# The end of an attention stage, written out as one sequence per engine, in a one-core Trainium2 kernel

## The chip, the cores and the metric

The kernel runs on one core of one Trainium2 chip. The metric is the device time of one execution in microseconds; the median of 3 runs of the kernel before is 155.03 us (154.98 to 155.16). The profiled execution is a fourth one, with its own time.

## The reference

A transformer block over 8 batches of 128 tokens of 256 floats: normalise, attend (8 heads), add, normalise again, route each token to one of 8 experts, and add the routed and a shared feed-forward layer.

```
x = x + attention(layernorm(x), ctx, ctx, lengths)
    # x is (8, 128, 256): the 128 rows are 8 heads of 16, the 256 columns are queries and keys
    # per batch and head: softmax(scale * log(length) * q^T k) applied to v
x = x + shared(layernorm(x)) + gate * expert(layernorm(x))
```

There are 64 heads in all (8 batches of 8), and each head's scores are a 256 by 256 matrix with an inner size of 16.

## The kernel before

Every engine has its own instruction list; semaphores order them. The attention is a software pipeline over steps `t`. In step t, up to 31, TensorE (PE) makes the raw scores of heads 2t and 2t+1 (`scores`, line 1021); VectorE (DVE) takes the maximum of each row of them (`maximum`, line 558). Seven steps later (`LAG`) PE makes the scores of the same two heads again, transposed and with the maximum subtracted (`shifted_scores`, line 1042), and ScalarE (ACT) takes the exponential out of PSUM (`exponentials`, line 813). PE then weighs the values of four heads, one half of the keys at a time (`weigh_values(m, c)`, line 1058). Every float32 matrix product is two matmul instructions, so that one call of `shifted_scores` (a head, one half of the keys) is two of them and one call of `weigh_values` is eight. A head's scores use 32 of the 128 rows of the PE array, and consecutive heads use different row groups; a head of the values uses 32 columns.

After the two halves of a batch's heads are weighed comes a chain that hands the batch from engine to engine: `copy_output` (ACT, 819), `turn_output` (PE, 1072), `scale_output` (DVE, 566 and 571), `turn_back` (PE, 1084), `add_attention` (DVE, 580), `token_stats` (DVE, 585 and 587), `token_rstd` (ACT, 823 and 825), `token_norm` (GpSimd, POOL, 428 and 431, for the batches up to 5; DVE, 591, for the last two), `turn_tokens` (PE, 1095), `high_tokens` (ACT, 829) and `low_tokens` (DVE, 596). `turn_output`, `turn_back` and `turn_tokens` of all batches but the last write one PSUM bank, X, so each waits until what the one before it left there has been read (`x_free`, which sorts them by the steps in OUT_TURN, OUT_BACK and TTURN). POOL also splits expert weights into high and low parts (`split_expert(n)`, lines 451 and 453), one of eight per step from t = 32 on.

Raw scores go through banks 0 to 2, shifted scores through banks 3 to 5 in turn. The raw scores end with t = 31, so that the steps from 32 to 39 hold the shifted scores of two heads each and no raw ones. One loop, `for t in range(TAIL)`, issues all steps on each engine; each looks up in lists by t which calls a step has. On PE the last steps are these: step 33 has `weigh_values(11, 1)`, shifted 52 and 53, `turn_tokens(3)`; 34 `weigh_values(12, 0)`, shifted 54 and 55, `turn_output(5)`; 35 `weigh_values(12, 1)`, 56 and 57, `turn_back(5)`; 36 `weigh_values(13, 0)`, 58 and 59, `turn_tokens(4)`; 37 `weigh_values(13, 1)`, 60 and 61, `turn_tokens(5)`; 38 `weigh_values(14, 0)`, 62 and 63, `turn_output(6)`; 39 `weigh_values(14, 1)`, (15, 0), (15, 1), `turn_back(6)`, `shared_up(0, 0)`; 40 `turn_output(7)`, `shared_up(0, 1)`; 41 `turn_tokens(6)`. The shared layer (`shared_up`, lines 1122 and 1123) and the experts follow.

Of the kernel before, what the change touches and what calls it, by code (L numbers as in the profile page):

```python
# [39 lines left out]
ACT = mybir.ActivationFunctionType  # L40
AX_X = mybir.AxisListType.X

P = 128
# [13 lines left out]
NS = 3  # L57
# [46 lines left out]
def tokens_at(shifted, offset, last):  # L104

    return shifted + [4 * b + offset for b in range(SHIFTED, B - 1)] + [END + last]
# [2 lines left out]
STATS = tokens_at([4 * b + LAG + 9 for b in range(SHIFTED)], LAG + 8, 7)  # L109
TRSTD = tokens_at([4 * b + LAG + 10 for b in range(SHIFTED)], LAG + 9, 8)  # L110
TNORM = tokens_at([4 * b + LAG + 11 for b in range(SHIFTED)], LAG + 9, 9)
TTURN = tokens_at([4 * b + LAG + 14 for b in range(SHIFTED - 1)] + [TURNS + 4], LAG + 10, 10)
THI, TLOW = TTURN, TTURN
TAIL = END + 3


SHARED_SPLIT = 14
# [37 lines left out]
def block_kernel(nc, x, ctx_in, lens, wg, w1, w3, w2, sw1, sw3, sw2, consts, out):  # L155
    with ExitStack() as es:
# [95 lines left out]


        bank = [es.enter_context(nc.psum_tensor(f"bank{i}", [P, 512], F32)) for i in range(8)]
        mx_bank, sc_bank, O, X = bank[0:NS], bank[NS:2 * NS], bank[6], bank[7]
        turned_out, back = X[:].rearrange("p (u h e) -> p u h e", u=2, h=H), X[:, 0:D]
        u1_bank, u3_bank = (bank[0], bank[3], bank[2]), (bank[1], bank[4], bank[5])
        eu1_bank, eu3_bank = (bank[3], bank[0]), (bank[4], bank[1])
# [134 lines left out]
        def _(pool):  # L393
# [49 lines left out]
            def split_expert(n):  # L443

                e, i = divmod(n, len(UP_PIECES))
                a, z = UP_PIECES[i]
                if i == 0:
                    pool.wait_ge(ld_w[e], 32)
                if n == 0:
                    pool.wait_ge(shifted, (B - 2) * H)  # L450
                nc.gpsimd.tensor_copy(ehi[e][:, a:z], whole[e][:, a:z]).then_inc(ew_hi_pool, 1)
                pool.wait_ge(ew_hi_pool, n + 1)
                nc.gpsimd.tensor_tensor(elo[e][:, a:z], whole[e][:, a:z], ehi[e][:, a:z].bitcast(F32),  # L453
                                        ALU.subtract).then_inc(ew_lo_pool, 1)

            for t in range(TAIL):
                for i, begin in LATE.items():
                    if t == begin:
                        for b in range(*CHUNKS[i]):
                            keys(b)  # L460
                    if t == begin + 1:
                        for b in range(*CHUNKS[i]):
                            queries(b, 0)
                            queries(b, 1)
                if t in TNORM[:B - 2]:
                    token_norm(TNORM.index(t))
                i, rest = divmod(t - SHARED_SPLIT, 3)
                if rest == 0 and 0 <= i < len(SHARED_PIECES):
                    split_shared(i)
                if 0 <= t - EXPERT_SPLIT < 2 * len(UP_PIECES):  # L470
                    split_expert(t - EXPERT_SPLIT)


            def send_rows(part):
# [35 lines left out]
        def _(dve):  # L510
# [143 lines left out]
                nc.vector.tensor_tensor(sig[k % 3][0:rows], u3_bank[UP_BANK[k]][0:rows, :], sig[k % 3][0:rows],  # L654
                                        ALU.mult).then_inc(h_made, 1)

            for t in range(TAIL):
                if t < TURNS:
                    maximum(2 * t)
                    maximum(2 * t + 1)  # L660
                if t == 1:
                    query_scales(1)
                    eager_queries(1)
                if t == LAG + 2:
                    nc.vector.tensor_copy(trib[:], cst[:, TRI:TRI + P]).then_inc(cst_copied, 1)
                    nc.vector.tensor_copy(x2[:, :, D:D + 1].bitcast(U32),
                                          cst[:, NUMBER:OWN].unsqueeze(2)).then_inc(numbered, 1)
                for i, begin in LATE.items():
                    if t == begin:
                        query_stats(i)  # L670
                    if t == begin + 1:
                        query_scales(i)
                for when, work in ((OUT_SCALE, scale_output), (OUT_ADD, add_attention), (STATS, token_stats),
                                     (TNORM[B - 2:], token_norm), (TLOW[:B - 2], low_tokens)):
                    if t in when:
                        work(when.index(t) + (B - 2 if work is token_norm else 0))
                if t == TURNS:
                    dve.wait_ge(v_turned, B // 2)
                    dve.wait_ge(k_eager, 2 * EAGER)
                    dve.wait_ge(k_made, 2 * (B - EAGER))  # L680
                    nc.vector.memset(lgt[3 * ROWS:P], 0.0).then_inc(lgt_set, 1)
# [36 lines left out]
            def expert_out(e):  # L718
# [2 lines left out]
                nc.vector.scalar_tensor_tensor(res[:, e, :], y_bank[(e + 1) % 2][:, 0:D], xe[:, e, D + 1:DW],  # L721
                                               res[:, e, :], ALU.mult, ALU.add).then_inc(e_out, 1)

            scale_output(B - 1)
            low_tokens(B - 2)
            add_attention(B - 1)
# [44 lines left out]
        def _(act):  # L771
# [36 lines left out]
            def exponentials(n):  # L808
                g = n // 4
                act.wait_ge(shifted, n + 1)  # L810
                if g >= NPT:
                    act.wait_ge(valued, g - NPT + 1)
                nc.scalar.activation(pt[:, g % NPT, n % 4, :], sc_bank[n % NS][:], ACT.Exp).then_inc(exped, 1)  # L813

            def copy_output(b):
                act.wait_ge(valued, 2 * b + 2)
# [49 lines left out]
            eager_keys(0)  # L866
            query_rstd(1)
            eager_keys(1)
            for t in range(TAIL):
                if t == MROW[0]:  # L870
                    maxima_rows(0)
                for i, begin in LATE.items():
                    if t == begin + 1:
                        query_rstd(i)
                if t in VALUES:
                    values(VALUES.index(t))
                if t in OUT_COPY:
                    copy_output(OUT_COPY.index(t))
                if 0 <= t - LAG < TURNS:
                    exponentials(2 * (t - LAG))  # L880
                if t in MROW[1:]:
                    maxima_rows(MROW.index(t))
                if t in THI[:B - 2]:
                    high_tokens(THI.index(t))
                if 0 <= t - LAG < TURNS:
                    exponentials(2 * (t - LAG) + 1)
                if t in TRSTD:
                    token_rstd(TRSTD.index(t))

            def expert_high(e, k):  # L890

# [66 lines left out]
        def _(pe):  # L958
# [74 lines left out]
            def shifted_scores(n, c):  # L1033

                b, half, rows = place(n)
                if n < NS and c == 0:
                    pe.wait_ge(maxed, FIRST - NS + n + 1)
                if n % H == 0 and c == 0:
                    pe.wait_ge(ld_m[b % 2], 32 * ring_pass(b, 2))
                if n >= NS and c == 0:  # L1040
                    pe.wait_ge(exped, n - NS + 1)
                mm = nc.tensor.matmul(sc_bank[n % NS][:, c * D:(c + 1) * D], kz[rows, b, half, c * P:(c + 1) * P],  # L1042
                                      qz[rows, b, half, :], start=True, stop=True)
                if c == 1:
                    mm.then_inc(shifted, 1)
# [108 lines left out]
                                          start=False, stop=(b == z - 2), skip_group_check=True)  # L1154
                mm.then_inc(pos_done, 1)

            for t in range(TAIL):
                if t == END + 1:
                    turn_output(B - 1)
                    shared_up(0, 1)  # L1160
                for m in range(NG):
                    for c in range(2):
                        if t == WEIGH[m][c]:
                            weigh_values(m, c)
                if t < LAG and t % 2 == 0:
                    first_half, heads = range(2), range(2 * t, min(2 * t + 4, 2 * LAG))
                    if t == 0:
                        for u in range(2):
                            for n in first_half:
                                scores(n, u)  # L1170
                        heads = range(2, 4)
                    for u in range(2):
                        for n in heads:
                            scores(n, u)
                for part in range(2):
                    for k in range(2):
                        if LAG <= t < TURNS:
                            scores(2 * t + k, part)
                        if 0 <= t - LAG < TURNS:
                            shifted_scores(2 * (t - LAG) + k, part)  # L1180
                if t == MROW[0]:
                    turn_maxima(0)
                if t in VALUES:
                    turn_values(VALUES.index(t))
                if t in UNREAD:
                    unread(t)
                for when, work in ((MROW[1:], turn_maxima), (OUT_TURN, turn_output), (OUT_BACK, turn_back),
                                     (TTURN, turn_tokens)):
                    if t in when:
                        work(when.index(t) + (1 if work is turn_maxima else 0))  # L1190

                if t == END:
                    shared_up(0, 0)

            def shared_down(b):

# [63 lines left out]
            def expert_down(e):  # L1260
# [10 lines left out]
                                          start=(c == 0), stop=(c == FC - 1))  # L1271
                mm.then_inc(e_down, 1)

            turn_back(B - 1)
            shared_up(1, 0)
            shared_up(1, 1)
# [50 lines left out]
```

## Time and profile before

| | |
|---|---|
| median of 3 runs | 155.03 us (154.98 to 155.16) |
| profiled execution, own time | 156.0 us |
| span of the profile | 154.1 us |
| busy: PE, DVE, ACT, POOL | 143.4, 99.3, 82.7, 67.2 us |
| the last shifted scores and values | about 71 to 86 us of the span |

The span runs from the first to the last instruction; the execution's own time is 1.9 us more. Busy time of PE is modelled by the ends of pipelined matmuls, so a full PE row says that it always had work begun, not that it worked at its peak. The kernel's pace is read from the starts of consecutive instructions.

### The profile page before, as it was taken

Reading aid. Unit: us, or ns where it says so; the run is one execution under the profiler, and the core shown is the slowest. Engines: PE = TensorE matmul, PEld = TensorE weight load, DVE = VectorE, ACT = ScalarE, POOL = GpSimd, SP = SyncE. Lnnn points to the kernel's source line nnn. Section 1 sums busy time; section 2 is a strip of 40 time slices with the busy share of each in tenths; the row PEclk is TensorE's granted clock in tenths of the full one; section 3 lists DMA queues with packets and bytes.
Section 4 is the critical chain, followed back from the end, with each engine's and each line's share of the span. In section 5 each row is a group of like instructions: output and inputs, shape, how many; then the busy total and the mean of one; then the engine's idle time right before and its main releaser. Section 6 shows DMA issues by size and latency. Waiting matters only on the chain.

```text
span 154.1 us, 3410 instructions
## 1 busy us (share of the span) xinstructions
PE 143.4 (93%) x1254; PEld 97.1 (63%) x1254; DVE 99.3 (64%) x232; ACT 82.7 (54%) x179; POOL 67.2 (44%) x100
## 2 busy tenths in 40 slices
PE   7799999998999999999998999999999999899930
PEld 2364565553655555555544677688999998899720
DVE  0589886688878888884232456887674484875220
ACT  3444265765848595767676248554503665762300
POOL 7115849303830508071639600276600777272350
PEclk9999999999999999999999999999999999999996
DMA  2992635362353500000800089722467532121010
GB/s 71 354 359 89 169 118 185 104 194 93 85 200 110 170 6 0 2 6 2 277 3 4 2 271 338 239 102 70 154 194 182 172 92 67 34 94 37 33 62 34
DMA packets 15824, 18.42 MB, mean 120 GB/s; under 512 B 1980, under 2 KB 15077, under 8 KB 15808
## 3 DMA queue, kind: packets, MB, share of 16 engines
q1 hardware_dynamic: 14368, 14.98, 30.6%
q0 software_dynamic: 1152, 2.97, 5.9%
q10 hardware_dynamic: 288, 0.26, 0.6%
q8 instruction: 10, 0.16, 0.4%
q14 instruction: 6, 0.05, 0.1%
HBM read 14.12 MB, written 4.21 MB: 119 GB/s over the span
## 4 chain that ended last, share of the span: by engine, by line
PE 84%; DVE 4%; issue 3%; DMA 2%; ACT 2%; POOL 2%; SPq 0%; DVEq 0%; POOLq 0%
PE bank L1021 19%; PE bank L1058 11%; PE bank L1210 6%; PE bank L1122 6%; PE bank L1042 6%; PE bank L1269 6%; PE bank L1123 5%; PE bank L1245 5%; PE bank L1244 4%; PE bank L973 3%; PE bank L1072 3%; DMA xs<-in_x 2%; PE bank L1084 2%; PE bank L1095 2%; PE bank L1030 2%
## 5 line engine op out<-in xcount | busy, mean ns | idle before, releaser
L558 DVE TENSOR_REDUCE nm<-bank 128x2 f32<-128x512 f32 x64 | 40.9, 686 | 10.0 <-PE bank L1021 9.5
L813 ACT ACTIVATE pt<-bank 128x512 f32<-128x512 f32 x64 | 36.2, 596 | 19.4 <-PE bank L1042 19.1
L1042 PE MATMUL bank<-qz,kz 32*128 32x256 f32 x256 | 37.9, 400 | 0.0
L1021 PE MATMUL bank<-kz,qz 32*128 32x256 f32 x256 | 34.6, 400 | 1.1 <-DVE qz L535 1.1
L1021 PEld LDWEIGHTS bank<-kz,qz 32*128 32x128 f32 x256 | 21.9, 184 | 13.5 <-DVE nm L558 5.8
L1042 PEld LDWEIGHTS bank<-qz,kz 32*128 32x128 f32 x256 | 23.5, 184 | 3.4 <-ACT pt L813 2.2
L1058 PE MATMUL bank<-pt,vext 128*32 128x256 f32 x256 | 20.2, 390 | 0.1
L403 POOL TENSOR_SCALAR qz<-xs,rs,mrs 128x256 f32<-128x256 f32 x14 | 7.7, 560 | 20.1 <-DVE mrs L529 20.1
L482 POOL DMA_INDIRECT expert_rows<-rk,idx_s x8 | 8.7, 1090 | 14.7 <-DVE idx_s L635 12.9
L497 POOL DMA_INDIRECT xs<-out,rk x8 | 8.8, 1099 | 11.1 <-DMA out<-xs 9.0
L504 POOL DMA_INDIRECT out<-xs,rk x8 | 8.4, 1048 | 11.3 <-DVE xs L721 6.9
L428 POOL TENSOR_SCALAR mrs<-mv,rstd 128x1 f32<-128x1 f32 x6 | 1.6, 260 | 23.4 <-ACT rstd L825 23.4
L973 PE MATMUL bank<-onesb 128*128 128x512 bf16 x34 | 10.7, 450 | 1.0 <-POOL onesb L397 1.0
L1058 PEld LDWEIGHTS bank<-pt,vext 128*32 128x32 f32 x256 | 5.2, 108 | 7.1 <-issue 5.7
L596 DVE TENSOR_TENSOR xlo<-bank,xhi 128x256 fp32r<-128x256 f32 x8 | 3.4, 422 | 8.1 <-ACT xhi L829 8.1
L715 DVE TENSOR_TENSOR qz_rest<-bank,late 128x352 f32<-128x352 f32 x8 | 4.2, 522 | 6.0 <-ACT late L919 4.7
L1269 PE MATMUL bank<-wraw,kz_rest 128*128 128x256 f32 (+1 forms) x30 | 7.4, 384 | 0.5 <-DVE rlo L708 0.5
L919 ACT ACTIVATE late<-bank 128x352 f32<-128x352 f32 x8 | 3.7, 466 | 7.6 <-PE bank L1245 6.9
L453 POOL TENSOR_TENSOR ew<-wraw,ew 128x352 fp32r<-128x352 f32 x8 | 7.5, 934 | 0.7
L973 PEld LDWEIGHTS bank<-onesb 128*128 128x128 bf16 x34 | 3.4, 112 | 5.9 <-issue 3.6
L1210 PE MATMUL bank<-shi,hThi 128*128 128x256 f32 (+1 forms) x24 | 7.0, 293 | 0.1
L1210 PE MATMUL bank<-shi,hTlo 128*128 128x256 f32 (+1 forms) x24 | 6.8, 282 | 0.0
(153 smaller groups left out, 301.3 us busy)
## 6 DMA issues: line engine op xcount, KB each, us to landing
wraw<-in_w SPq DMA_DIRECT2D x10, 352.0 KB, 3.4
wlate<-in_w SPq DMA_DIRECT2D x6, 352.0 KB, 4.2
wraw<-in_w SPq DMA_DIRECT2D x10, 128.0 KB, 3.4
expert_rows<-zero SPq DMA_DIRECT2D x1, 1032.0 KB, 6.7
out<-xs SPq DMA_DIRECT2D x8, 128.0 KB
xs<-in_x SPq DMA_DIRECT2D x3, 256.0 KB, 4.9
cs<-in_ctx SPq DMA_DIRECT2D x3, 256.0 KB, 5.1
wlate<-in_w SPq DMA_DIRECT2D x6, 128.0 KB, 3.9
```

The costliest lines, as they stand in the source:

```text
L482: nc.gpsimd.indirect_dma_start(xd_dram, bass.IndirectOffsetOnAxis(ap=idx_s[:, b:b + 1], axis=0), x2[:, b, :], None, bounds_check=E * C - 1 ...
L497: nc.gpsimd.indirect_dma_start(res[:, e, :], None, out_rows, number(e), bounds_check=B * P - 1, oob_is_err=False).then_inc(gathered[e], 16)
L504: nc.gpsimd.indirect_dma_start(out_rows, number(e), res[:, e, :], None, bounds_check=B * P - 1, oob_is_err=False).then_inc(out_sent, 16)
L558: nc.vector.tensor_reduce(nm[:, b % 2, :, place], scores_bank[:].rearrange("p (u c) -> p u c", u=2), AX_X, ALU.max, negate=True).then_inc( ...
L813: nc.scalar.activation(pt[:, g % NPT, n % 4, :], sc_bank[n % NS][:], ACT.Exp).then_inc(exped, 1)
L973: nc.tensor.matmul(X[:].rearrange("p (n c) -> p n c", c=P), onesb[:], onesb[:].unsqueeze(1).broadcast_to([P, 4, P]), start=True, stop=True)
L1021: mm = nc.tensor.matmul(scores_bank[:, u * D:(u + 1) * D], qz[rows, b, half, u * P:(u + 1) * P], kz[rows, b, half, :], start=True, stop=True)
L1042: mm = nc.tensor.matmul(sc_bank[n % NS][:, c * D:(c + 1) * D], kz[rows, b, half, c * P:(c + 1) * P], qz[rows, b, half, :], start=True, sto ...
L1058: mm = nc.tensor.matmul(O[32 * j:32 * j + 32, g * D:(g + 1) * D], vext[:, b, c, h, :], pt[:, m % NPT, i, c * D:(c + 1) * D], start=(c == 0 ...
L1122: nc.tensor.matmul(u1, weights(part, S1 + f * P, F + WG, c, n1), tokens, start=a, stop=z)
L1210: mm = nc.tensor.matmul(base_bank[b % 2][:, 0:D], hpart[0:rows, half, f, j * P:(j + 1) * P], part[0:rows, S2 + f * D:S2 + (f + 1) * D], st ...
L1269: mm = nc.tensor.matmul(y_bank[(e + 1) % 2][:, 0:D], hTe[0:rows, e % 2, c * P:(c + 1) * P], down_at[e][c][0:rows], start=(c == 0), stop=(c ...
```

## The change

The step loops of all engines now end after step 32 (`STEADY`). What came after is written out call by call for PE, ACT, DVE and POOL. On PE the last twelve heads' shifted scores (52 to 63) are issued in three groups of four heads, first half of the keys of all four, then the second half; they use the banks 4, 1, 2, 0, 5, 3 in turn, so banks of the raw scores too. The key halves of the values of groups 13, 14 and 15 of four heads stand together. On POOL `split_expert(1)` to `(6)` come ahead of `token_norm(4)`. `turn_tokens(5)` comes after `turn_back(6)`.

```diff
-TTURN = tokens_at([4 * b + LAG + 14 for b in range(SHIFTED - 1)] + [TURNS + 4], LAG + 10, 10)
+TTURN = [4 * b + LAG + 14 for b in range(SHIFTED - 1)] + [TURNS + 4, END + 1, END + 2]
-TAIL = END + 3
+STEADY = TURNS + 1
+FOURS = 2 * (STEADY - LAG)
+FOURS_BANKS = (4, 1, 2, 0, 5, 3)
+def shifted_bank(n):
+    return NS + n % NS if n < FOURS else FOURS_BANKS[(n - FOURS) % len(FOURS_BANKS)]
+def banks_last_head(n):
+    return next((k for k in range(n - 1, -1, -1) if shifted_bank(k) == shifted_bank(n)), None)
...
 # POOL, after the loop
+            for n in range(1, 7):
+                split_expert(n)
+            token_norm(B - 4)
+            split_expert(7)
+            token_norm(B - 3)
...
 # DVE, after the loop
+            low_tokens(3)
+            scale_output(5)
+            add_attention(5)
+            token_stats(5)
+            low_tokens(4)
+            scale_output(6)
+            add_attention(6)
+            token_stats(6)
+            low_tokens(5)
+            token_norm(6)
             scale_output(B - 1)
             low_tokens(B - 2)
...
 # ACT, after the loop
+            copy_output(5)
+            exponentials(52)
+            high_tokens(3)
+            exponentials(53)
+            exponentials(54)
+            exponentials(55)
+            token_rstd(4)
+            exponentials(56)
+            exponentials(57)
+            copy_output(6)
+            token_rstd(5)
+            exponentials(58)
+            high_tokens(4)
+            for n in range(59, NH):
+                exponentials(n)
+            token_rstd(6)
+            high_tokens(5)
+            copy_output(B - 1)
...
 # PE, in shifted_scores
-                if n >= NS and c == 0:
-                    pe.wait_ge(exped, n - NS + 1)
+                last = banks_last_head(n)
+                if last is not None and c == 0:
+                    pe.wait_ge(exped, last + 1)
+                if n >= FOURS and shifted_bank(n) < NS and c == 0:
+                    pe.wait_ge(maxed, NH)
...
+            def four_shifted(n):
+                for part in range(2):
+                    for k in range(4):
+                        shifted_scores(n + k, part)
...
 # PE, after the loop
+            weigh_values(11, 1)
+            four_shifted(52)
+            turn_tokens(3)
+            weigh_values(12, 0)
+            turn_output(5)
+            weigh_values(12, 1)
+            four_shifted(56)
+            turn_back(5)
+            weigh_values(13, 0)
+            weigh_values(13, 1)
+            turn_tokens(4)
+            four_shifted(60)
+            turn_output(6)
+            weigh_values(14, 0)
+            weigh_values(14, 1)
+            turn_back(6)
+            turn_tokens(5)
+            weigh_values(15, 0)
+            weigh_values(15, 1)
+            shared_up(0, 0)
+            turn_output(B - 1)
+            shared_up(0, 1)
+            turn_tokens(6)
             turn_back(B - 1)
```

## Rows read from the trace of the kernel before

**Rows 1.** The page: the chain that ended last, by engine.
```profile
PE 84%; DVE 4%; issue 3%; DMA 2%; ACT 2%; POOL 2%; SPq 0%; DVEq 0%; POOLq 0%
```

**Rows 2.** PE in order of time, the tail: start, duration, what, idle before it.
```profile
71.30 1.13 PE L1042 MATMUL bank<-qz,kz 32*128 32x256 f32 x8
72.36 0.44 PE L1095 MATMUL bank<-cst,rk 128*128 128x128 f32 x2
72.74 0.64 PE L1058 MATMUL bank<-pt,vext 128*32 128x256 f32 x8
73.31 1.13 PE L1042 MATMUL bank<-qz,kz 32*128 32x256 f32 x8
74.37 0.66 PE L1072 MATMUL bank<-cst,osum 128*128 128x128 f32 x4
74.96 0.64 PE L1058 MATMUL bank<-pt,vext 128*32 128x256 f32 x8
...
81.54 0.44 PE L1095 MATMUL bank<-cst,rk 128*128 128x128 f32 x2 [0.88 <-POOL rk L431]
...
85.78 0.44 PE L1084 MATMUL bank<-cst,att 128*128 128x128 f32 x2
85.97 0.48 PE L1122 MATMUL bank<-xhi,shi 128*104 128x512 f32 x1
...
87.47 0.60 PE L1072 MATMUL bank<-cst,osum 128*128 128x128 f32 x4
```

**Rows 3.** The same list in a steady step: first score matmul, and what follows all 16.
```profile
65.11 0.48 PE L1021 MATMUL bank<-kz,qz 32*128 32x256 f32 x1
...
66.19 0.55 PE L1072 MATMUL bank<-cst,osum 128*128 128x128 f32 x3
```

**Rows 4.** The chain that ended last: start, duration, what; the last two value halves.
```profile
84.78 1.07 PE bank L1058 x16
```

**Rows 5.** ACT in order of time in the tail.
```profile
72.96 0.37 ACT L829 CAST xhi<-bank 128x256 fp32r<-128x256 f32 x1
73.21 0.62 ACT L813 ACTIVATE pt<-bank 128x512 f32<-128x512 f32 x1
...
74.47 1.09 ACT L813 ACTIVATE pt<-bank 128x512 f32<-128x512 f32 x2 [0.22 <-PE bank L1042]
...
79.92 0.31 ACT L823 ACTIVATE lnv<-mv,epst 128x1 f32<-128x1 f32 x1
...
80.37 0.57 ACT L819 COPY osum<-bank 128x512 f32<-128x512 f32 x1
80.84 0.60 ACT L813 ACTIVATE pt<-bank 128x512 f32<-128x512 f32 x1
...
85.92 0.59 ACT L819 COPY osum<-bank 128x512 f32<-128x512 f32 x1 [1.19 <-PE bank L1058]
```

**Rows 6.** DVE in order of time in the tail.
```profile
73.36 0.42 DVE L596 TENSOR_TENSOR xlo<-bank,xhi 128x256 fp32r<-128x256 f32 x1 [1.91 <-ACT xhi L829]
...
75.36 0.42 DVE L571 TENSOR_TENSOR att<-bank,rinv 128x256 f32<-128x256 f32 x1
...
86.26 0.42 DVE L580 TENSOR_TENSOR xs<-bank,xs 128x256 f32<-128x256 f32 x1 [1.30 <-PE bank L1084]
```

**Rows 7.** POOL in order of time: two weight splits, and one norm of tokens.
```profile
67.04 0.48 POOL L451 CAST ew<-wraw 128x352 fp32r<-128x352 f32 x1
...
68.48 0.47 POOL L451 CAST ew<-wraw 128x352 fp32r<-128x352 f32 x1
...
80.57 0.26 POOL L428 TENSOR_SCALAR mrs<-mv,rstd 128x1 f32<-128x1 f32 x1 [2.44 <-ACT rstd L825]
80.93 0.56 POOL L431 TENSOR_SCALAR rk<-xs,rstd,mrs 128x256 f32<-128x256 f32 x1
```

**Rows 8.** Busy time by stretch: length, each engine's busy us, PE clock, DMA.
```profile
80.00:82.00 2.00, 1.12 (x14) 0.53 (x14) 0.01 (x1) 1.41 (x5) 1.25 (x4) 1.00 0.00 0
...
140.00:154.00 14.00, 7.62 (x42) 6.40 (x40) 2.84 (x6) 1.81 (x4) 3.89 (x4) 0.92 0.11 37
```

More of the change, by code:

```diff
@@ L254, in block_kernel @@
         bank = [es.enter_context(nc.psum_tensor(f"bank{i}", [P, 512], F32)) for i in range(8)]
-        mx_bank, sc_bank, O, X = bank[0:NS], bank[NS:2 * NS], bank[6], bank[7]
+        O, X = bank[6], bank[7]
         turned_out, back = X[:].rearrange("p (u h e) -> p u h e", u=2, h=H), X[:, 0:D]
@@ L454, in split_expert @@
                                         ALU.subtract).then_inc(ew_lo_pool, 1)
-            for t in range(TAIL):
+            for t in range(STEADY):
                 for i, begin in LATE.items():
@@ L471, in _ @@
                     split_expert(t - EXPERT_SPLIT)
+            for n in range(1, 7):
[3 more added lines that the diff above has]
+            token_norm(B - 3)
+            for n in range(8, 2 * len(UP_PIECES)):
+                split_expert(n)
             def send_rows(part):
@@ L655, in shared_hidden @@
                                         ALU.mult).then_inc(h_made, 1)
-            for t in range(TAIL):
+            for t in range(STEADY):
                 if t < TURNS:
@@ L812, in exponentials @@
                     act.wait_ge(valued, g - NPT + 1)
-                nc.scalar.activation(pt[:, g % NPT, n % 4, :], sc_bank[n % NS][:], ACT.Exp).then_inc(exped, 1)
+                nc.scalar.activation(pt[:, g % NPT, n % 4, :], bank[shifted_bank(n)][:], ACT.Exp).then_inc(exped, 1)
             def copy_output(b):
@@ L868, in _ @@
             eager_keys(1)
-            for t in range(TAIL):
+            for t in range(STEADY):
                 if t == MROW[0]:
@@ L1039, in shifted_scores @@
                     pe.wait_ge(ld_m[b % 2], 32 * ring_pass(b, 2))
-                if n >= NS and c == 0:
-                    pe.wait_ge(exped, n - NS + 1)
-                mm = nc.tensor.matmul(sc_bank[n % NS][:, c * D:(c + 1) * D], kz[rows, b, half, c * P:(c + 1) * P],
+                last = banks_last_head(n)
[3 more added lines that the diff above has]
+                    pe.wait_ge(maxed, NH)
+                mm = nc.tensor.matmul(bank[shifted_bank(n)][:, c * D:(c + 1) * D], kz[rows, b, half, c * P:(c + 1) * P],
                                       qz[rows, b, half, :], start=True, stop=True)
@@ L1155, in count_tokens @@
                 mm.then_inc(pos_done, 1)
[L1157 to L1160, printed above, removed]
+            for t in range(STEADY):
                 for m in range(NG):
@@ L1190, in _ @@
                         work(when.index(t) + (1 if work is turn_maxima else 0))
-                if t == END:
-                    shared_up(0, 0)
+            def four_shifted(n):
+                for part in range(2):
+                    for k in range(4):
+                        shifted_scores(n + k, part)
             def shared_down(b):
```

## The prediction

> **What bounds the kernel now.** I read the page first, for the engine that carries the chain of waits. The reader is to see that PE holds 84% of it and the DMA 2% [rows 1]: what shortens PE's list, or its idle time, shortens the kernel, as long as nothing else becomes late. Then I read the instructions in order of time, engine by engine, from 70 to 88 us, since averages over the kernel say nothing about this stretch. In it PE is never without work but once: it stands 0.88 us before `turn_tokens(5)` for POOL's normed tokens [rows 2]. The other engines wait for it: the exponentials of two heads take ACT 1.09 us [rows 5], while the two heads' scores and what stands between them and the next pair take PE about 2 us (71.30 to 73.31, 73.31 to 75.53) [rows 2].
>
> The step of most weight is a ratio of two rows. In the tail one pair of heads is 8 matmul instructions and takes 72.36 - 71.30 = 1.06 us [rows 2]. In a steady step 16 instructions (two raw, two shifted heads, in four row groups) take 66.19 - 65.11 = 1.08 us [rows 3]. PE runs as many row groups at once as it is given, and the tail gives it two of four.
>
> **The change part by part.** All times are on the span's own scale; differences of starts are used, not durations, because matmuls overlap.
>
> *Shifted scores.* Six pairs at 1.06 = 6.36 us go, three groups of four come. The trace has no group of four shifted heads. From below a group costs no less than the pair's 1.06, from above two pairs, 2.12. I take 1.08, the steady step, which has the same shapes, the same four row groups and four banks [rows 3]. Gain 3.12 us of PE work.
>
> *Key halves together.* One half with its neighbours is 75.53 - 74.96 = 0.57 us [rows 2]; the last two, which stand together already, take 85.78 - 84.78 = 1.00 [rows 2, 4]. Groups 13 and 14 come together: 2 x (1.14 - 1.00) = 0.28 us less. Their bounds are 0 and 0.28; I take 1.00 for each.
>
> *The turns.* As many as before: `turn_output` 74.96 - 74.37 = 0.59, `turn_tokens` and `turn_back` 0.38 (72.74 - 72.36) [rows 2]. They are what is late next, since the chain that hands a batch from engine to engine has not become shorter and PE now comes to its links earlier. So the gain isn't the sum of the two terms above, and I lay the new order out from 71.30, where both kernels start their first tail scores.
>
> First group 71.30 to 72.38; `turn_tokens(3)` to 72.75; values (12, 0) to 73.32. `turn_output(5)` waits for `low_tokens(3)`. That chain begins with the first exponential, 1.18 us after the group's start (a pair's is 74.47 - 73.31 = 1.16 [rows 2, 5], four heads end some hundredths later), so at 72.48; `high_tokens(3)` 0.49 later (an exponential's share of the 1.09 [rows 5]) at 72.97; `low_tokens(3)` 0.40 after that (73.36 - 72.96) and 0.42 long [rows 5, 6]: 73.79. With 0.05 for the hand-over to PE (as 81.54 after 80.93 + 0.56 [rows 2, 7]) PE goes on at 73.84: **first gap 0.52**.
>
> `turn_output(5)` to 74.43, values (12, 1) to 75.00, second group to 76.08 (heads 56 to 59 wait for exponentials up to 53, over by 74.2, and for the maxima of batch 7, sent in the last loop step), `turn_back(5)` to 76.46, values 13 to 77.46. `turn_tokens(4)` waits for POOL. POOL's second split starts at 68.48; a split takes 68.48 - 67.04 = 1.44; six of them now stand ahead of `token_norm(4)`, which takes 0.92 (80.57 to 81.49) [rows 7]. So 68.48 + 6 x 1.44 + 0.92 + 0.05 = 78.09: **second gap 0.63**. `token_rstd(4)` is over by 75.3 (exponentials 52 to 55 and one copy from 72.48), so the splits, and not ACT, are the price here. Behind the waiting `turn_tokens(4)` stand the last group and all values; ACT waits for neither then, as it still has exponentials 58 and 59.
>
> `turn_tokens(4)` to 78.47, last group to 79.55. On ACT: exponential 56 at 76.18, 57 at 76.67, `copy_output(6)` 1.14 after values 13 began (85.92 - 84.78 [rows 4, 5]), at 77.60, 0.47 long to its follower, `token_rstd(5)` 0.45 (80.37 - 79.92 [rows 5]), exponential 58 at 78.52, `high_tokens(4)` at 79.01, `low_tokens(4)` done at 79.83. `turn_output(6)` at 79.88: **third gap 0.33**. It ends at 80.47, values 14 at 81.47; the scaled output is ready 1.41 after the turn's start (75.36 + 0.42 - 74.37 [rows 2, 6]), at 81.29, in time. `turn_back(6)` 81.47. `turn_tokens(5)` now stands right behind it in the same bank and must wait for `add_attention(6)`, 0.48 later (86.26 - 85.78) and 0.42 long [rows 2, 6], with the hand-over 82.42: **fourth gap 0.57**. To 82.80; values 15 to 83.80 (exponential 63 is over at 81.8: five at 0.49 from 79.26, and 0.60).
>
> `shared_up(0, 0)` then takes 87.47 - 85.97 = 1.50 [rows 2], so `turn_output(7)` starts at 85.30 (`copy_output(7)`, 1.14 after 82.80, is over at 84.5) against 87.47: **2.2 us earlier**. The same sum as a balance: PE work falls by 3.12 + 0.28, less 0.06 for rounding and a `turn_back` that no longer overlaps its follower; the one gap of 0.88 goes and four of 2.05 together come: about 2.2.
>
> *Waits added.* A group in a bank of the raw scores waits for the last maximum; the DVE's maxima end with step 31 and the first group is in step 33. Priced at nothing; had it to wait, everything on PE would. *POOL* ends its splits before 81, where it ended them at 87.2; the experts need them 30 us later. *After the tail* the order is the same on each engine, and expert loads, sends, stores and gathers all hang on instructions of the PE list (the load of expert 5 on `turn_output(7)`), so they move with it. I carry the whole 2.2 to the end.
>
> *A rule of the skill.* The exponentials, copies and norms of the tail are, from 72.48, 12 x 0.49 + 2 x 0.25 + 2 x 0.45 + 0.47 = 7.75 us of ACT (the `high_tokens` step is 73.21 - 72.96 [rows 5]), so ACT alone would be through at 80.3 and PE, waiting only for it, at 81.3. The Trainium skill (TensorEngine Tiling, "PSUM Bottleneck") says that after a fourfold tiling speed-up the copies out of PSUM may become the bound. By that rule ACT sets the tail and the kernel would gain about 4 us; by the rows ACT idles and the batch's chain sets it. No sum above uses the rule.
>
> **Time.** The profiled execution took 156.0 us with a span of 154.1; its outside part, 1.9, doesn't change, so it would be 153.8. The median shown is 155.03, 1.0 below that execution, and on this scale the forecast is 155.03 - 2.2 = 152.8 us.
>
> **The rivals.**
>
> *The gaps are hidden.* If the four links come in time, PE's own work sets the tail: 2.05 less idle, up to 150.8; with half of them 151.8. For it: each gap is 0.3 to 0.6 us, made of hand-overs that I added one by one. Against: they are rows, not guesses, and POOL's has one fixed start.
>
> *Given back later.* A transfer that doesn't move with PE (gathers, stores, weights of experts 5 to 7) takes half: 153.9. For it: the last 14 us have PE busy for only 7.62 [rows 8]. Against: DMA is 2% of the chain [rows 1].
>
> *The change doesn't do what it says.* Shifted heads don't run four wide, and a group costs 2.12. Laid out the same way the gap before `turn_output(5)` stays 0.5, POOL's is covered, the one before `turn_tokens(5)` stays, and values 15 end at about 85.9: 155.0, no change. Against: the steady step [rows 3].
>
> *Slower.* Four gaps in 9 us make PE's clock fall from 2.4 to 1.2 GHz (granted clock 1.00 to 0.5). From the second gap on, 78 to 84 us, 4.8 us of work would cost 4.8 more: 157.6. It decides once more than 2.2 us of work run at half rate. For it: where PE is busy for about half of 14 us the granted clock's mean is 0.92 [rows 8]. The Trainium skill (TensorE: Matmul & The Clock Gate, "What's actually happening") says that throttled is the default state and activity releases it. Against: a stretch with 0.88 of 2.00 us idle kept 1.00 [rows 8], and no new gap is as long.
>
> **How the numbers follow.** Forecast 0.70 (own range 152.3 to 153.3), gaps hidden 0.11, given back 0.09, not four wide 0.04, slower by the clock 0.05, other 0.01. The range, 151.8 to 154.1, takes in the forecast, half of the gaps hidden and half of the gain given back. A measurement of this kernel tells 0.2% (0.3 us) from no change. Faster 0.90, same 0.05, slower 0.05.
>
> **What would show it.** Right: three lots of 16 shifted matmul instructions, each about 1.08 us to PE's next start; PE idle before four turns, released by DVE, POOL, DVE, DVE, by 0.5, 0.6, 0.3 and 0.6; `token_norm(4)` at about 77.1; `turn_output(7)` at 85.3. Wrong: a group near 2 us, a granted clock under 1.00 between 76 and 90, or a chain of waits that leaves PE for DMA after 110 us.

## The result, and the profile after

The changed kernel takes 153.03 us (median of 4, 152.96 to 153.07) against 155.01 us for the kernel before (154.98 to 155.16): 1.98 us less, ratio 0.986 with a 95% interval of 0.9826 to 0.9893. Forecast were 152.8 us and a gain of 2.2. Times scattered on the occasion of the first four experiments below (the kernel before took 155.19 to 161.04 us there), so those four are judged by the length of the tail in their profile and not by their median. The profiled execution took 153.0 us, its span is 151.1.

PE in order of time, the changed kernel's tail (start, duration, what, idle before it). The same list of the kernel before is in [rows 2].

```profile
70.59 0.64 PE L1110 MATMUL bank<-pt,vext 128*32 128x256 f32 x8
71.16 1.15 PE L1094 MATMUL bank<-qz,kz 32*128 32x256 f32 x16
72.24 0.44 PE L1147 MATMUL bank<-cst,rk 128*128 128x128 f32 x2
72.61 0.64 PE L1110 MATMUL bank<-pt,vext 128*32 128x256 f32 x8
73.79 0.63 PE L1124 MATMUL bank<-cst,osum 128*128 128x128 f32 x4 [0.54 <-DVE xlo L616]
...
77.95 0.44 PE L1147 MATMUL bank<-cst,rk 128*128 128x128 f32 x2 [0.51 <-POOL rk L443]
78.31 1.15 PE L1094 MATMUL bank<-qz,kz 32*128 32x256 f32 x16
79.86 0.63 PE L1124 MATMUL bank<-cst,osum 128*128 128x128 f32 x4 [0.41 <-DVE xlo L616]
80.42 1.07 PE L1110 MATMUL bank<-pt,vext 128*32 128x256 f32 x16
81.42 0.44 PE L1136 MATMUL bank<-cst,att 128*128 128x128 f32 x2
82.47 0.41 PE L1147 MATMUL bank<-cst,rk 128*128 128x128 f32 x2 [0.61 <-DVE xs L600]
82.81 1.07 PE L1110 MATMUL bank<-pt,vext 128*32 128x256 f32 x16
...
85.29 0.60 PE L1124 MATMUL bank<-cst,osum 128*128 128x128 f32 x4
```

The reader is to see three things. A group of four heads is 16 matmul instructions in 72.24 - 71.16 = 1.08 us, where two heads took 1.06 [rows 2]. PE stands before four turns, released by DVE, POOL, DVE, DVE. And `turn_output(7)` starts at 85.29, 14.13 us after the first tail group, against 87.47 - 71.30 = 16.17 [rows 2]: 2.04 us less, which is the whole measured gain.

The rows that set these four releases, DVE and POOL in order of time:

```profile
73.22 0.42 DVE L616 TENSOR_TENSOR xlo<-bank,xhi 128x256 fp32r<-128x256 f32 x1 [1.91 <-ACT xhi L859]
...
79.29 0.42 DVE L616 TENSOR_TENSOR xlo<-bank,xhi 128x256 fp32r<-128x256 f32 x1 [1.72 <-ACT xhi L859]
...
81.90 0.42 DVE L600 TENSOR_TENSOR xs<-bank,xs 128x256 f32<-128x256 f32 x1 [0.65 <-PE bank L1136]
```

```profile
76.98 0.26 POOL L440 TENSOR_SCALAR mrs<-mv,rstd 128x1 f32<-128x1 f32 x1
77.33 0.56 POOL L443 TENSOR_SCALAR rk<-xs,rstd,mrs 128x256 f32<-128x256 f32 x1
```

The stretch that holds the first gap and the one that holds the other three (length, PE, PE load, DVE, ACT, POOL busy, granted clock, DMA share, GB/s) both keep a granted clock of 1.00, the 2.4 GHz level, as the stretch with the old gap did [rows 8]:

```profile
70.00:75.00 5.00, 4.46 (x56) 2.00 (x52) 2.03 (x6) 4.43 (x11) 4.68 (x8) 1.00 0.27 75
76.00:90.00 14.00, 12.47 (x111) 8.06 (x108) 6.06 (x19) 8.10 (x21) 3.89 (x7) 1.00 0.29 91
```

After the tail, the chain that ended last (start, duration, what; first the kernel before, then the changed one). The prediction named a chain that leaves PE for DMA after 110 us as a sign of being wrong, and the chain does that here: DMA has 4% of it now, against 2% before. The first expert rows land just as PE gets to them. But PE's own wait for them is short (the last row below: 0.15 us), and the stretch from the first `shared_down` to `turn_rows(0)` is not longer: 115.03 - 107.05 = 7.98 us before, 112.71 - 104.87 = 7.84 after.

```profile
107.05 4.47 PE bank L1210 x36
111.58 3.45 PE bank L1210 x27
115.03 0.37 PE bank L1225 x2
...
129.23 0.48 DVE xs L721
129.71 1.19 issue
130.90 0.44 DVE rlo L708
```

```profile
104.87 4.49 PE bank L1262 x36
...
110.60 2.06 DMA rk<-expert_rows
112.71 0.44 PE bank L1277 x2
```

```profile
112.71 0.44 PE L1277 MATMUL bank<-cst,rk 128*128 128x128 f32 x2 [0.15 <-DMA rk<-expert_rows]
```

The spans differ by 3.0 us and not by 2.0. Of the other 1.0 us, 0.14 lies ahead of the tail (`weigh_values(11, 1)` starts at 70.73 before and 70.59 after) and 0.8 behind it, in the experts: the profiled execution of before has 1.19 us in its chain in which DVE waited for nothing that the profile shows, and was itself 1.0 us over the median. From `turn_output(7)` to the end of the span it took 66.6 us, the changed kernel 65.8. Profiles of other kernels below show either length (65.8 to 66.3, or 66.8), whatever was edited, so this isn't the change's.

### The profile page after: what moved, and what is told of

It reads as the page before. It is cut to its first block, busy times and chain, and to the rows that moved or that the text cites. A ratio compares the mean times of both kernels' runs of the same rounds, so it can differ in the third digit from the quotient of the medians.

```text
span 151.1 us, 3413 instructions
## 1 busy us (share of the span) xinstructions
PE 139.9 (93%) x1254; PEld 95.4 (63%) x1254; DVE 99.3 (66%) x232; ACT 82.1 (54%) x179; POOL 67.9 (45%) x100
## 4 chain that ended last, share of the span: by engine, by line
PE 83%; DVE 4%; DMA 4%; issue 3%; ACT 2%; POOL 1%; SPq 0%; ACTq 0%; POOLq 0%; DVEq 0%
PE bank L1070 20%; PE bank L1110 11%; PE bank L1321 6%; PE bank L1174 6%; PE bank L1175 6%; PE bank L1297 5%; PE bank L1296 5%; PE bank L1262 4%; PE bank L1094 4%; PE bank L1022 3%; PE bank L1124 3%; DMA xs<-in_x 2%; PE bank L1136 2%; PE bank L1079 2%; PE bank L1308 2%
## 5 line engine op out<-in xcount | busy, mean ns | idle before, releaser
L843 ACT ACTIVATE pt<-bank 128x512 f32<-128x512 f32 x64 | 35.6, 597 | 17.4 <-PE bank L1094 17.3
L1094 PE MATMUL bank<-qz,kz 32*128 32x256 f32 x256 | 34.6, 400 | 0.0
L1094 PEld LDWEIGHTS bank<-qz,kz 32*128 32x128 f32 x256 | 21.6, 184 | 1.7 <-ACT pt L843 1.0
L517 POOL DMA_INDIRECT xs<-out,rk x8 | 9.9, 1235 | 12.0 <-DMA out<-xs 9.8
```

The lines of the kernel that those rows point to most:

```text
L517: nc.gpsimd.indirect_dma_start(res[:, e, :], None, out_rows, number(e), bounds_check=B * P - 1, oob_is_err=False).then_inc(gathered[e], 16)
L843: nc.scalar.activation(pt[:, g % NPT, n % 4, :], bank[shifted_bank(n)][:], ACT.Exp).then_inc(exped, 1)
L1094: mm = nc.tensor.matmul(bank[shifted_bank(n)][:, c * D:(c + 1) * D], kz[rows, b, half, c * P:(c + 1) * P], qz[rows, b, half, :], start=Tru ...
```

## The experiments

Each row of this table is one profile and one series of times. "Tail" runs from the start of `weigh_values(11, 1)` to the start of `turn_output(7)` on PE, "rest" from there to the end of the span. The first four experiments (two_wide to gaps_closed) are judged by the tail, the others by both. The last column compares with the kernel before as it ran on the same occasion, and not with the 155.01 us of the first row.

| kernel | tail, us | rest, us | median, us | against before (95%) |
|---|---|---|---|---|
| before | 87.47 - 70.73 = 16.74 | 66.6 | 155.01 | |
| changed | 85.29 - 70.59 = 14.70 | 65.8 | 153.03 | 0.986 (0.9826 to 0.9893) |
| two_wide | 85.48 - 70.78 = 14.70 | 66.8 | 153.46 | 0.975 (0.970 to 0.980) |
| fours_alone | 85.21 - 70.77 = 14.44 | 66.0 | 153.08 | 0.974 (0.969 to 0.980) |
| norm_early | 85.42 - 70.72 = 14.70 | 66.8 | 153.73 | 0.977 (0.971 to 0.983) |
| gaps_closed | 83.65 - 70.60 = 13.05 | 66.3 | 152.02 | 0.966 (0.961 to 0.971) |
| changed_again | 85.35 - 70.64 = 14.71 | 66.0 | 153.08 | 0.985 (0.982 to 0.989) |
| pairs_apart | 86.98 - 70.73 = 16.25 | 65.9 | 154.69 | 0.996 (0.994 to 0.998) |
| waits_swapped | 85.09 - 70.58 = 14.51 | 66.1 | 152.98 | 0.985 (0.981 to 0.988) |
| tokens5_late | 84.50 - 70.61 = 13.89 | 66.0 | 152.24 | 0.980 (0.976 to 0.983) |
| gaps_closed_again | 83.55 - 70.49 = 13.06 | 65.9 | 151.44 | 0.974 (0.969 to 0.978) |
| chain_first | 83.24 - 70.60 = 12.64 | 65.9 | 151.06 | 0.974 (0.968 to 0.980) |

**changed_again** is the changed kernel itself on another occasion.

> The changed kernel, unedited, as the common base of these runs. Both theories: from the start of weigh_values(11, 1) to turn_output(7) 14.70 us, as in its first profile; 153.0 us if nothing after the tail is late.

It repeated its tail within 0.01 us and its time within 0.05.

### Does the width carry the gain?

**two_wide**, each group as two pairs directly behind each other:

```diff
             def four_shifted(n):
-                for part in range(2):
-                    for k in range(4):
-                        shifted_scores(n + k, part)
+                for first in (n, n + 2):
+                    for part in range(2):
+                        for k in range(2):
+                            shifted_scores(first + k, part)
```

> Theory (the width of the shifted scores carries the gain): with two heads at a time in the same places a group costs 2 x 1.06 = 2.12 us instead of 1.08, three groups 3.1 us more PE work, of which POOL's gap before turn_tokens(4) and part of the one before turn_output(6) are covered: 2.1 us slower than the changed kernel, about 155.0 us. Rival (the order and the value halves carry it): within 0.5 us of 153.0.

The expectation failed, and by its number the rival was right: the tail is that of the changed kernel. PE in order of time shows why:

```profile
71.35 1.16 PE L1094 MATMUL bank<-qz,kz 32*128 32x256 f32 x16
72.44 0.44 PE L1147 MATMUL bank<-cst,rk 128*128 128x128 f32 x2
```

The 16 instructions took 1.09 us, not 2.12. The edit had not made them two wide: the second pair uses the other two row groups and ran beside the first without being interleaved with it. A stretch of 0.15 us at the start of the group (71.25 to 71.40) has four of them under way, all begun in it:

```profile
71.35 0.51 PE L1094 MATMUL bank<-qz,kz 32*128 32x256 f32 x4
```

So the run left the question open.

**pairs_apart**, the same pairs with a turn or a half of values between them:

```diff
-            four_shifted(52)
+            two_shifted(52)
             turn_tokens(3)
+            two_shifted(54)
...
+            two_shifted(56)
             weigh_values(12, 1)
-            four_shifted(56)
+            two_shifted(58)
...
+            two_shifted(60)
             turn_tokens(4)
-            four_shifted(60)
+            two_shifted(62)
```

> The changed kernel with each group of four taken apart into two pairs with a turn or a half of values between them (52, 53 / turn_tokens(3) / 54, 55; 56, 57 / weigh_values(12, 1) / 58, 59; 60, 61 / turn_tokens(4) / 62, 63). Theory (what saves the time is that 16 matmul instructions over four row groups follow each other, in whatever order): a pair alone costs 1.06 again, turn_output(7) starts 1.9 us later than in the changed kernel (16.6 after weigh_values(11, 1)), about 154.9 us. Rival (a group's saving comes from elsewhere, such as fewer exchanges with ACT): within 0.5 us of the changed kernel, as two adjacent pairs were.

PE in order of time:

```profile
71.30 1.13 PE L1094 MATMUL bank<-qz,kz 32*128 32x256 f32 x8
72.36 0.44 PE L1147 MATMUL bank<-cst,rk 128*128 128x128 f32 x2
72.73 1.13 PE L1094 MATMUL bank<-qz,kz 32*128 32x256 f32 x8
73.80 0.64 PE L1110 MATMUL bank<-pt,vext 128*32 128x256 f32 x8
74.37 0.66 PE L1124 MATMUL bank<-cst,osum 128*128 128x128 f32 x4
```

A pair takes 72.36 - 71.30 = 1.06 again, and the kernel 154.69 us, 1.61 more than the changed one beside it (tail 1.54 more; 1.9 was expected). The 3.1 us of additional PE work fill the gaps that the changed kernel has, all but the one before `turn_tokens(5)`: there is none before `turn_output(5)` here. In the same 0.15 us at its start a pair has two instructions under way, where two_wide has four:

```profile
71.30 0.48 PE L1094 MATMUL bank<-qz,kz 32*128 32x256 f32 x2
```

That four heads next to each other make the groups cheap is shown, and the order within the group doesn't matter. The banks that the pairs use are those of the change, so that the new banks alone don't give the gain. But each head has both a row group and a bank of its own, and no run parts the two: that it is the row groups and not the four banks written side by side is my reading. Two adjacent pairs in the same row groups, which would tell, were not tried. Against the kernel before, the new order with pairs is still 0.49 us shorter in the tail (16.25 against 16.74).

**fours_alone** takes the groups of four and leaves all other calls, on all engines, in the order of the kernel before:

```diff
 # POOL
-            for n in range(1, 7):
-                split_expert(n)
-            token_norm(B - 4)
-            split_expert(7)
-            token_norm(B - 3)
-            for n in range(8, 2 * len(UP_PIECES)):
+            split_expert(1)
+            token_norm(4)
+            split_expert(2)
+            split_expert(3)
+            token_norm(5)
+            for n in range(4, 8):
                 split_expert(n)
...
 # PE
             weigh_values(13, 0)
+            turn_tokens(4)
             weigh_values(13, 1)
-            turn_tokens(4)
             four_shifted(60)
+            turn_tokens(5)
+            weigh_values(14, 0)
             turn_output(6)
-            weigh_values(14, 0)
             weigh_values(14, 1)
-            turn_back(6)
-            turn_tokens(5)
             weigh_values(15, 0)
             weigh_values(15, 1)
+            turn_back(6)
             shared_up(0, 0)
...
 # and ACT's and DVE's calls in the order of the kernel before
```

> Groups of four and their banks, with all other calls of ACT, DVE and POOL in the order of the kernel before, and PE's turns and values as there too. Theory (the width alone carries the gain, the rest of the new order is worth nothing): laid out from the rows, PE stands before turn_output(5) by 0.6, before turn_tokens(5) and turn_output(6) by 0.6 and 0.5, turn_output(7) starts within 0.3 of the changed kernel's 85.3: 152.9 us (152.6 to 153.3). Rival (the new order is needed to make use of the groups): 154 us or more.

PE in order of time, from the third group on:

```profile
78.12 1.15 PE L1093 MATMUL bank<-qz,kz 32*128 32x256 f32 x16
80.07 0.44 PE L1146 MATMUL bank<-cst,rk 128*128 128x128 f32 x2 [0.81 <-POOL rk L443]
80.44 0.64 PE L1109 MATMUL bank<-pt,vext 128*32 128x256 f32 x8
81.52 0.63 PE L1123 MATMUL bank<-cst,osum 128*128 128x128 f32 x4 [0.44 <-DVE xlo L616]
82.08 1.50 PE L1109 MATMUL bank<-pt,vext 128*32 128x256 f32 x24
83.51 0.44 PE L1135 MATMUL bank<-cst,att 128*128 128x128 f32 x2
```

The theory holds, and more than that: the tail is 0.26 us shorter than with the whole change. It has three gaps (0.54, 0.81, 0.44) where the whole change has four. The four-head groups carry all of the gain, and by the tails the new order of the rest costs a little beside them. The medians (153.08 us here, 153.03 and 153.08 for the changed kernel on other occasions) don't tell the two apart.

### What are the gaps worth?

**norm_early**, POOL's `token_norm(4)` after split 4:

```diff
-            for n in range(1, 7):
+            for n in range(1, 5):
                 split_expert(n)
             token_norm(B - 4)
-            split_expert(7)
+            for n in range(5, 8):
+                split_expert(n)
...
```

> The changed kernel with POOL's token_norm(4) after split 4 and not after split 6. Theory: the gap before turn_tokens(4) goes (0.5 us), but turn_output(6) waits for low_tokens(4), which hangs on copy_output(6), token_rstd(5) and exponential 58 on ACT, not on POOL: its gap grows from 0.4 to 1.0 and the time stays at 153.0 (within 0.1). Rival (each gap of PE is worth its length): 152.5.

PE in order of time:

```profile
77.50 0.44 PE L1146 MATMUL bank<-cst,rk 128*128 128x128 f32 x2
77.86 1.15 PE L1093 MATMUL bank<-qz,kz 32*128 32x256 f32 x16
79.99 0.63 PE L1123 MATMUL bank<-cst,osum 128*128 128x128 f32 x4 [0.99 <-DVE xlo L615]
```

The turn starts without a gap, `turn_output(6)` waits 0.99 instead of 0.41, and the tail stays at 14.70. The median, 153.73, missed the expected 153.0: the tail bears the theory out, the time doesn't. The gap that was removed is worth nothing in the tail, since the next one hangs on another engine's list.

**tokens5_late**, `turn_tokens(5)` after `shared_up(0, 0)`:

```diff
             turn_back(6)
-            turn_tokens(5)
             weigh_values(15, 0)
             weigh_values(15, 1)
             shared_up(0, 0)
+            turn_tokens(5)
             turn_output(B - 1)
...
 # ACT
+            copy_output(B - 1)
             token_rstd(6)
             high_tokens(5)
-            copy_output(B - 1)
```

> The changed kernel with turn_tokens(5) after shared_up(0, 0) and copy_output(7) ahead of token_rstd(6) on ACT. Theory: only the gap before turn_tokens(5) goes (0.68 us), values 15 start right behind turn_back(6) as exponential 63 is just over; with a cheaper place for the turn turn_output(7) starts 0.8 us earlier: 152.2 us. Rival: the gap moves to values 15 or to turn_output(7) and the time stays at 153.0.

PE in order of time:

```profile
81.44 0.44 PE L1136 MATMUL bank<-cst,att 128*128 128x128 f32 x2
81.80 1.07 PE L1110 MATMUL bank<-pt,vext 128*32 128x256 f32 x16
```

Values 15 follow `turn_back(6)` at once. The tail is 0.82 us shorter, the time 0.84: as laid out. This gap came with the change's own order, two links of the chain directly behind each other.

**gaps_closed** moves all links ahead of what can wait:

```diff
 # ACT
             copy_output(5)
-            exponentials(52)
             high_tokens(3)
-            exponentials(53)
-            exponentials(54)
-            exponentials(55)
+            for n in range(52, 56):
+                exponentials(n)
...
             copy_output(6)
+            high_tokens(4)
+            for n in range(58, NH):
+                exponentials(n)
             token_rstd(5)
-            exponentials(58)
-            high_tokens(4)
-            for n in range(59, NH):
-                exponentials(n)
...
 # PE
             weigh_values(11, 1)
+            turn_tokens(3)
             four_shifted(52)
-            turn_tokens(3)
...
 # and the edits of norm_early and tokens5_late
```

> The links of the batch's chain ahead of what can wait: PE turn_tokens(3) before the first group, turn_tokens(5) after shared_up(0, 0); ACT high_tokens(3) before exponential 52, high_tokens(4) before 58, token_rstd(5) after 63; POOL token_norm(4) after split 4. Theory (the chain sets the tail, laid out again from the rows): gaps of about 0.1, 0, 0.15 and 0.5 (exponential 63), turn_output(7) 1.7 us earlier: 151.4 us (151.1 to 151.8). Rival (something after the tail has a time of its own, a load or a store): less than half of it, 152.3 or more.

PE in order of time:

```profile
80.11 0.44 PE L1132 MATMUL bank<-cst,att 128*128 128x128 f32 x2
80.95 1.07 PE L1106 MATMUL bank<-pt,vext 128*32 128x256 f32 x16 [0.40 <-ACT pt L842]
```

The tail fell by 1.65 us, 1.7 were expected. The median, 152.02, was above the expected range on that occasion; **gaps_closed_again**, the same kernel on another, settled it:

> The kernel with the links of the chain first, unedited, as the base of the next one. Its first profile had 13.05 us from weigh_values(11, 1) to turn_output(7), 1.65 less than the changed kernel; the changed kernel's 153.0 less 1.65 is 151.4 us. Rival (part of the gain is lost after the tail): 151.8 or more.

It took 151.44 us, with a tail of 13.06. Nothing is lost behind the tail. Now ACT's last exponential ends the wait of values 15: ACT has become the engine that PE waits for longest.

### The hand-over to PE

In the changed kernel PE went on 0.15 us after DVE's end (73.79 against 73.22 + 0.42) and 0.06 after POOL's (77.95 against 77.33 + 0.56). **waits_swapped** exchanges the two waits in `turn_output` and `turn_tokens`:

```diff
             def turn_output(b):
-                pe.wait_ge(o_copied, b + 1)
                 if b < B - 1:
                     x_free("output", b)
+                pe.wait_ge(o_copied, b + 1)
 # and in turn_tokens x_free before pe.wait_ge(x2_made, b + 1)
```

> The changed kernel with the two waits of turn_output and of turn_tokens in the other order (first for the bank X, then for the data). PE went on 0.15 us after the end of DVE's last instruction at turn_output(5), turn_output(6) and turn_tokens(5), and 0.06 after POOL's at turn_tokens(4). Theory A (the second of two waits is released late): the three become 0.06 and POOL's becomes 0.15, 0.2 us less in the tail, 152.8. Theory B (it is the DVE instruction that reads PSUM whose end is signalled later): all stay as they are, 153.0.

PE, DVE and POOL at the first and the second gap, in order of time (PEld is the weight load):

```profile
73.20 0.42 DVE L616 TENSOR_TENSOR xlo<-bank,xhi 128x256 fp32r<-128x256 f32 x1 [1.91 <-ACT xhi L859]
...
73.69 0.55 PE L1124 MATMUL bank<-cst,osum 128*128 128x128 f32 x3 [0.45 <-DVE xlo L616]
...
77.32 0.56 POOL L443 TENSOR_SCALAR rk<-xs,rstd,mrs 128x256 f32<-128x256 f32 x1
...
77.99 0.20 PEld L1147 LDWEIGHTS bank<-cst,rk 128*128 128x128 f32 x2 [1.12 <-issue]
78.02 0.30 PE L1147 MATMUL bank<-cst,rk 128*128 128x128 f32 x1 [0.67 <-POOL rk L443]
```

Theory A holds: DVE's hand-over is now 73.69 - 73.62 = 0.07, POOL's 78.02 - 77.88 = 0.14 (PE's two other gaps that DVE ends give 0.06 each). The wait that stands second is the slower one for both: first it was the one for the bank, which DVE releases, now it is the one for the data, which POOL releases. The tail lost 0.20 us as computed; the median only 0.10, which the runs' own spread covers.

**chain_first** adds the swapped waits to gaps_closed, and puts exponential 58 in an idle place of ACT:

```diff
             exponentials(57)
+            exponentials(58)
             copy_output(6)
             high_tokens(4)
-            for n in range(58, NH):
+            for n in range(59, NH):
...
 # and on PE the waits of turn_output and turn_tokens as in waits_swapped
```

> The same with exponential 58 ahead of copy_output(6) on ACT, in the 0.33 us in which ACT waits for the copy, and with the waits of the turns in the swapped order. Theory: exponential 63 is over 0.4 us earlier and the gap of 0.40 before values 15 goes, turn_output(6) comes 0.05 to 0.1 earlier by the waits: 0.4 to 0.5 us less, 150.9 us (150.8 to 151.1), the tail 12.6 us. Rival (the copy is later by as much as the exponential takes and the whole chain with it): 151.4 or more.

The tail is 12.64 us and the time 151.06, against 12.6 and 150.9. It is 0.38 us faster than gaps_closed_again beside it, 2.0 faster than the changed kernel and about 4 faster than the kernel before (155.01 - 151.06 = 3.95). One of its six times is 152.82 us, which is why its ratio in the table is no lower than that of gaps_closed_again; the tails differ by 0.42. The run has two edits, and what each is worth alone was not measured.

## Why the prediction was right

**Shifted scores.** A group of four cost 1.08 us, the value taken from the steady step. The price was right. Its reason, that PE runs as many row groups at once as it is given, left open what "given" means, and the first experiment took it to be the order within the group. two_wide and pairs_apart show that it is which heads' instructions stand next to each other, in whatever order.

**Key halves together.** An adjacent half costs 0.43, one that stands alone 0.57 (24 instructions in 83.51 - 82.08 = 1.43 in fours_alone, that is 0.57 + 2 x 0.43). The Trainium skill (TensorEngine Tiling, "Key Properties") says that a change of the tiling mode drains the engine. If that is the cause here, it cost 0.14 us each time; no run tests it. The term has two parts of 0.14 us. In the changed kernel that of group 13 ends ahead of the wait for POOL, whose end doesn't depend on it, so it is worth nothing: the balance at the end of the working lists it as a gain and has it again in a second gap that is longer by as much. That of group 14 lies between the third gap and `turn_back(6)`, where the layout did count it. No run takes it out alone. In fours_alone (14, 0) stands alone, but (14, 1), (15, 0) and (15, 1) run through at 1.43, which saves the same 0.14 in another place.

**The turns.** All four gaps came, in the forecast order and with the forecast releasers. From the end of the work before to PE's start they were 0.61, 0.59, 0.47 and 0.68 (worked from the same starts: 73.79 less 72.61 + 0.57, and so on), against 0.52, 0.63, 0.33 and 0.57. The step that was mis-sized is the hand-over of 0.05 us, which I had from the one row of POOL [rows 2, 7] and used for DVE's three too, where it is 0.15. The first of these 0.10 us is taken up by the wait for POOL, which ends at its own time: `turn_tokens(4)` starts 6.79 us after the first group, as laid out. The other two make 0.20; the rest of the layout came out 0.07 shorter (a turn behind a gap takes 0.56 and 0.34, not 0.59 and 0.38). So the tail is 14.13 us instead of 14.00. It is 0.13 of the 0.2 us by which the gain was smaller than forecast; the rest is within what one profile and medians differ by.

Two sums of the working are loose without moving the forecast. The balance takes the old gap at 0.88 us, its idle time on the page; from start to start, as all else there is measured, it is 81.54 less 79.53 + 1.06 = 0.95, so the 0.06 "for rounding" stands for more than rounding. And exponential 63 is four steps and not five behind the start of 59; the 81.8 is right (81.71 measured).

**POOL.** `token_norm(4)` began at 76.98, forecast 77.1, held back by the six splits. But it wasn't the price that I called it: norm_early shows 0.00 us for it, since ACT's list (the copy, the rstd and exponential 58 ahead of `high_tokens(4)`) has `turn_output(6)` wait until the same moment.

**After the tail** the gain was carried whole: the tail fell by 2.04 us and the time by 1.98. With each kernel that is judged by both, the time moved as the tail did, within 0.1 us. The sign of being wrong that the prediction named, DMA in the chain after 110 us, did come, but it costs PE 0.15 us of waiting in a stretch that is no longer than before. As a sign it was poorly chosen: the chain shows who came last, and not by how much.

**The rivals.** "The gaps are hidden" did not happen by itself and takes an order of its own: chain_first gives 151.06 us, where 151.8 was priced for half of the gaps and 150.8 for all. "Given back later" forecast 153.9 us; with 1.98 of the tail's 2.04 us in the time, nothing of that size was given back. "Not four wide" was real at 154.69 for pairs that are truly apart, against 155.0 forecast. "Slower by the clock" did not occur: granted clock 1.00 through all four gaps. The Trainium skill's rule (TensorEngine Tiling, "PSUM Bottleneck"), by which the copies out of PSUM may become the bound, did not decide the changed kernel: exponential 63 was over at 81.71 and values 15 began at 82.81, and no gap of PE is released by ACT directly. It began to in gaps_closed (0.40 us for exponential 63). By the prediction's own rows that rival was worth 4.7 us and not "about 4" (`turn_output(7)` at 81.3 + 1.5 against 87.47); chain_first, with the links in another order, has 4.1 of it.

## What to carry to other kernels

When small matmuls use a part of the array's rows, put those of different row groups next to each other in PE's list, each with a PSUM bank of its own as here; two short groups with a turn between them cost twice one long group. Then lay the dependent chain through the shorter list link by link: it gives the gain that remains, and shows which gap is worth nothing because another engine's list makes PE wait until the same moment anyway. Links that other engines wait for go ahead of bulk work, and bulk work goes between two links.

## What the runs showed of the hardware

Of two waits ahead of a PE instruction, the late one costs less when it stands first. In the changed kernel the data's wait stands first and the bank's second: late data cost 0.06 us from the releaser's end, a late bank 0.15. In waits_swapped it is the other way round: late bank 0.06 to 0.07, late data 0.14. Why, the traces don't show.

Two pairs of heads in different row groups (and different banks) overlapped fully (1.09 us for 16 instructions) although the first pair's eight instructions all stood before the second's.
